# First stage of a fused attention and expert layer on one core: three rounded products in place of plain fp32, value rows spread over the chunks, statistics and norms reordered

## The reference

```
xn = (x - mean) / sqrt(var + 1e-5)
q, k, v = xn @ Wq.T, xn @ Wk.T, xn @ Wv.T          # 16 heads of 16 columns
attn = softmax(q k^T / 16) v                       # all 4096 x 4096 pairs of each head
scores = softmax(xn @ gate_w.T); idx = top2(scores + gate_b)
y = sum over the 2 experts of scores[idx] * expert_idx(xn);  z = shared expert(xn)
expert(x) = silu((x @ w1 + b1) * (x @ w3 + b3)) @ w2 + b2      # 352 hidden columns
out = x + attn + y + z
```

## Time and profile before

| what | value |
|---|---|
| median of 3 runs | 2173.07 us |
| profiled execution, its own time | 2174.21 us |
| its span | 2172.3 us |
| granted TensorE clock, mean | 0.996 of full |
| TensorE (PE) busy | 2152.4 us, 99% |
| ScalarE (ACT) busy | 2009.4 us, 93% |
| VectorE (DVE) busy | 800.5 us, 37% |
| GpSimd (POOL) busy | 246.0 us, 11% |

### The profile page before, as it was taken

The page is one execution under the profiler, slowest core; times in us unless marked ns, Lnnn a source line. Parts: engine busy times, 40 slices in busy tenths (PEclk is TensorE's granted clock), DMA queues, the critical chain, the costliest instruction groups (busy, mean ns, idle before and its releaser), DMA issues.

```text
span 2172.3 us, 37982 instructions
## 1 busy us (share of the span) xinstructions
PE 2152.4 (99%) x15638; PEld 965.2 (44%) x15638; DVE 800.5 (37%) x1515; ACT 2009.4 (93%) x2209; POOL 246.0 (11%) x242
## 2 busy tenths in 40 slices
PE   9999999999999999999999999999999999999998
PEld 4632344444444444444444444444444444444322
DVE  6321143344344334334334434334334334544200
ACT  4599999999999999999999999999999999999998
POOL 0100465610000000000000000000000002223200
PEclk9999999999999999999999999999999999999999
DMA  7671334332222222213132222213213222332120
GB/s 254 206 280 33 91 121 130 100 90 66 63 78 63 76 57 79 78 54 85 48 77 70 77 64 69 78 50 83 75 50 90 63 69 75 105 97 66 57 78 3
DMA packets 223595, 187.24 MB, mean 86 GB/s; under 512 B 112039, under 2 KB 194558, under 8 KB 223166
## 3 DMA queue, kind: packets, MB, share of 16 engines
q1 hardware_dynamic: 211598, 149.41, 24.3%
q0 software_dynamic: 11824, 35.40, 5.0%
HBM read 130.21 MB, written 54.53 MB: 85 GB/s over the span
## 4 chain that ended last, share of the span: by engine, by line
PE 92%; ACT 7%; DVE 1%; DMA 0%; issue 0%; DVEq 0%
PE PS L672 41%; PE PS L659 29%; PE PS L684 12%; ACT probs L866 6%; PE PS L695 6%; PE PS L565 2%; PE PS L602 1%; PE PS L575 0%; DVE stats L972 0%; PE PS L554 0%; DMA resid<-in_x 0%; DVE probs L996 0%; ACT probs L818 0%; DVE o_t L1169 0%; DVE mv L975 0%
## 5 line engine op out<-in xcount | busy, mean ns | idle before, releaser
L866 ACT ACTIVATE probs<-PS 128x1024 f32<-128x1024 f32 x2048 | 1920.0, 1080 | 96.0 <-PE PS L659 81.8
L672 PE MATMUL PS<-probs,v_head 128*32 128x512 f32 x8192 | 1002.8, 601 | 1.1 <-ACT probs L866 0.8
L659 PE MATMUL PS<-q_ring,k_stack 50*128 50x512 f32 x4096 | 741.3, 446 | 7.0 <-ACT probs L866 6.2
L659 PEld LDWEIGHTS PS<-q_ring,k_stack 50*128 50x128 f32 x4096 | 332.6, 185 | 627.2 <-ACT probs L866 569.6
L672 PEld LDWEIGHTS PS<-probs,v_head 128*32 128x32 f32 x8192 | 206.6, 108 | 448.2 <-issue 359.6
L1194 DVE TENSOR_SCALAR gate_in<-PS,bias_sb 128x256 f32<-128x256 f32 x165 | 79.6, 482 | 754.9 <-PE PS L684 739.5
L684 PE MATMUL PS<-x_hi,w_hi 128*128 128x256 f32 (+1 forms) x660 | 201.3, 305 | 0.0
L684 PE MATMUL PS<-x_hi,w_lo 128*128 128x256 f32 (+1 forms) x660 | 186.5, 283 | 0.0
L684 PE MATMUL PS<-x_lo,w_hi 128*128 128x256 f32 (+1 forms) x660 | 185.6, 281 | 0.0
L921 POOL DMA_DIRECT2D slot_y<-y_sb x39 | 27.9, 716 | 1285.1 <-DVE y_sb L1262 1251.6
L684 PEld LDWEIGHTS PS<-x_hi,w_hi 128*128 128x128 f32 (+1 forms) x660 | 118.6, 180 | 60.0 <-issue 60.0
(11 more groups left out here) (137 smaller groups left out, 1098.2 us busy)
## 6 DMA issues: line engine op xcount, KB each, us to landing
w_raw<-in_w SPq DMA_DIRECT2D x110, 352.0 KB
k_stack<-qk_parts SPq DMA_DIRECT2D x120, 128.0 KB
w_raw<-in_w SPq DMA_DIRECT2D x55, 256.0 KB
q_ring<-qk_parts SPq DMA_DIRECT2D x384, 32.0 KB
slot_x<-part_a SPq DMA_DIRECT2D x39, 256.0 KB, 2.3
slot_in<-slot_x SPq DMA_DIRECT2D x156, 64.0 KB, 2.4
slot_y<-y_sb POOLq DMA_DIRECT2D x39, 256.0 KB, 2.5
k_stack<-qk_parts SPq DMA_DIRECT2D x136, 64.0 KB
```

The source lines that it names most:

```text
L659: last = pe.matmul(bank(2 * score_buffer(turn, g) + r), k_stack[rows, kt * P:(kt + 1) * P], q_ring[rows, sweep, i * QC:(i + 1) * QC], star ...
L672: last = pe.matmul(bank(O_BANK)[VW * j:VW * (j + 1), :], v_head[:, kt, :], probs[:, slot, (j % 2) * QC:(j % 2 + 1) * QC], start=(kt == 0), ...
L866: nc.scalar.activation(probs[:, prob_slot(g), :], bank(2 * score_buffer(h, g), 2), ACT.Exp, scale=ENERGY_SCALE).then_inc(s_exp, 1)
```

## The change

**Formats.** Chunk 0 is still projected in fp32 (`first_project`), the keys before chunk 1 is transposed and the queries after it. For chunks 1 to 7, ScalarE writes two copies of each transposed half: rounded (`xh`, a ring of four chunks) and exact (`xfull`, a ring of two); VectorE writes their difference (`xl`, in `tokens_low`). The weights are split once (`wqk_hi`, `wqk_lo`, `wvg_hi`, `wvg_lo`). A projection job is then six fp32r matmuls of 512 columns, the products high times high, high times low, and low times high over two halves of the features, in place of two fp32 matmuls. A pair of value rows is twelve fp32r matmuls of 264 columns in place of four in fp32.

**Order.** Keys come before queries. Chunks 1 to 3 do both; chunks 4 to 7 do keys alone, and their queries come after chunk 7 (`late_queries`). Value pairs 0 to 4 are done in chunks 1 to 3 in banks 0 and 1, which `turn_xn` also uses; pairs 5 to 9 in chunks 4 to 7 in banks 4 and 5; pairs 10 to 15 at the end. Query norms of the two halves of the chunks go to bank 6 and bank 5, and the shift is made and stored by halves. The statistics of group 2 are split in two groups, and statistics and normalisation are put behind the subtractions that other engines wait for.

**Transfers.** Keys and queries are stored separately, 512 KB a part. `xfull` is stored chunk by chunk (eight DMAs of 512 KB) in place of the one of 4 MB. Head 0's queries of the first sweep are loaded after chunk 7; its shift after the queries of chunk 7 are stored and before the flag. ScalarE's copy of pair 12 waits for the stores of the even chunks' queries.

```diff
+FIRST = NCH // 2
+PAIRS = NT // 2
+SIDE_PAIR = 5
+LATE_PAIR = 10
+LN_GROUPS = ((0, 4), (4, 8), (8, 12), (12, 16), (16, 24), (24, NT))
+LN_LOAD = (0, 1, 2, 2, 3, 4)
...
+def pair_bank(n):
+
+    if n < LATE_PAIR:
+        return 0 if n < SIDE_PAIR else 4
+    return 2 * ((n - LATE_PAIR) % 3)
+
+
+def late_bank(m):
+
+    return 2 + m % 3
...
+                sp.wait_ge(s_xt, DT * (c + 1))
+                sp.dma_start(x_rows[:, :, c * QC:(c + 1) * QC], xfull[:, c % 2, :, :]).then_inc(s_xd[c % 2], 16)
+                store_keys(c)
                 if c:
-                    sp.wait_ge(s_store[part_of(c - 1)], stored(c - 1))
+                    sp.wait_ge(s_kst[(c - 1) % 2], stored(c - 1))
                     load_k_chunk(c - 1)
-                if c == QCH:
-                    load_q_rows(0, 0)
-            sp.wait_ge(s_store[part_of(NCH - 1)], stored(NCH - 1))
+                if c < FIRST:
+                    store_queries(c)
+            for half in range(2):
+                sp.wait_ge(s_qst[half], stored(FIRST - 2 + half))
+            load_q_rows(0, 0)
+            store_queries(4)
+            store_queries(5)
+            sp.wait_ge(s_kst[(NCH - 1) % 2], stored(NCH - 1))
             load_k_chunk(NCH - 1)
-            for s in range(NP_):
-                sp.wait_ge(s_s1, s + 1)
-                sp.dma_start(qshift_parts[s].rearrange("h (c t) -> c h t", c=NCH), spart[:, s, :].bitcast(f32)).then_inc(s_sst, 16)
+            store_shift(0)
+            store_queries(6)
+            store_queries(7)
+            sp.wait_ge(s_sst, 16 * NP_)
+            load_q_shift(0, 0, s_q[0])
             sp.wait_ge(s_flag, 1)
             flag = sp.value_load(flag_i[0:1, 0:1], min_val=0, max_val=1)
...
+                    pe.wait_ge(s_xt, dt + 1)
+                    last = pe.matmul(bank(4 - 2 * w + i), wqk[:, w, dt, i * P:(i + 1) * P], cols, start=(dt == 0), stop=(dt == DT - 1))
...
+                hi, lo = xh[c % XRING], xl[c % XRING]
+                for dt in range(DT):
+                    pe.wait_ge(s_xh, DT * c + dt + 1)
+                    pe.matmul(bank(b), wqk_hi[:, w, dt, cols], moving(hi, dt), start=(dt == 0), stop=False)
+                    pe.matmul(bank(b), wqk_lo[:, w, dt, cols], moving(hi, dt), start=False, stop=False)
+                pe.wait_ge(s_xl, c + 1)
+                for dt in range(DT):
+                    last = pe.matmul(bank(b), wqk_hi[:, w, dt, cols], moving(lo, dt), start=False, stop=(dt == DT - 1))
+                last.then_inc(s_qk, 1)
+
+            def keys(c, i):
+
+                if c == 1 and i == 0:
+                    pe.wait_ge(s_wl, 1)
+                pe.wait_ge(s_res, key_job(c - 1) + i + 1)
...
+            def value_rows(n):
+
+                if n == 0:
+                    pe.wait_ge(s_vwl, 1)
+                if n < SIDE_PAIR or n == LATE_PAIR:
+                    pe.wait_ge(s_xt, DT * turned[0])
+                    pe.wait_ge(s_xh, DT * turned[0])
+                if n == SIDE_PAIR:
+                    pe.wait_ge(s_res, query_job(FIRST - 1) + DT)
+                if n == LATE_PAIR + 1:
+                    pe.wait_ge(s_res, NCH * NJ)
+                if n == LATE_PAIR + 2:
+                    pe.wait_ge(s_qn, 2)
+                if 0 < n <= LATE_PAIR:
+                    pe.wait_ge(s_vc, n)
+                if n >= LATE_PAIR + 3:
+                    pe.wait_ge(s_vc, n - 2)
+                for i in range(2):
+                    c, t = (2 * n + i) // TPC, (2 * n + i) % TPC
+                    rows = slice(t * P, (t + 1) * P)
                     for dt in range(DT):
-                        last = pe.matmul(bank(6 + w), hones_b[:, dt, own], sq[:, c % 2, w * DT + dt, :],
-                                         start=(c == 0 and dt == 0), stop=(c == NCH - 1 and dt == DT - 1))
-                last.then_inc(s_nr, 1)
+                        dst = bank(pair_bank(n) + i)[:, 0:VE]
+                        pe.matmul(dst, xh[c % XRING][:, dt, rows], wvg_hi[:, dt, :], start=(dt == 0), stop=False)
+                        pe.matmul(dst, xh[c % XRING][:, dt, rows], wvg_lo[:, dt, :], start=False, stop=False)
+                        last = pe.matmul(dst, xl[c % XRING][:, dt, rows], wvg_hi[:, dt, :], start=False, stop=(dt == DT - 1))
+                last.then_inc(s_v, 1)
...
             turn_first()
+            first_project(1, 0)
+            first_project(1, 1)
+            turn_xn(1)
+            first_project(0, 0)
+            first_project(0, 1)
             pe.wait_ge(s_hb, 2)
-            for c in range(NCH):
-                pe.wait_ge(s_xt, c + 1)
-                project(c, 0)
-                project(c, 1)
+            key_norms(0)
+            for c in range(1, FIRST):
+                keys(c, 0)
+                query_norms(c - 1)
+                keys(c, 1)
+                if c > 1:
+                    value_rows(2 * c - 3)
+                queries(c, 0)
+                turn_xn(c + 1)
+                queries(c, 1)
+                key_norms(c)
+                value_rows(2 * c - 2)
+            for c in range(FIRST, NCH):
+                keys(c, 0)
+                if c == FIRST:
+                    query_norms(FIRST - 1)
                 if c < NCH - 1:
                     turn_xn(c + 1)
-                if c:
-                    norms(c - 1)
-                project(c, 2)
-                project(c, 3)
...
-            value_rows(0)
+                if c == FIRST:
+                    value_rows(5)
+                keys(c, 1)
+                value_rows(c + 2)
+                key_norms(c)
+            late_queries(4, 0)
+            late_queries(4, 1)
             pe.wait_ge(s_mk, 1)
             pe.transpose(bank(7)[0:1, 0:P], kmax[:, 0:1], ident_sb[:, :]).then_inc(s_kt, 1)
-            value_rows(1)
+            late_queries(5, 0)
+            query_norms(4)
+            late_queries(5, 1)
             pe.wait_ge(s_krow, 1)
             pe.matmul(bank(7)[:, P:P + 1], krow[0:1, 0:P], ones_sb[0:1, 0:1], start=True, stop=True).then_inc(s_kb, 1)
-            value_rows(2)
-            value_rows(3)
-            value_rows(4)
+            late_queries(6, 0)
+            query_norms(5)
+            late_queries(6, 1)
+            late_queries(7, 0)
+            query_norms(6)
+            late_queries(7, 1)
+            value_rows(10)
+            query_norms(7)
+            value_rows(11)
             pe.wait_ge(s_gcol, 1)
             pe.transpose(bank(6)[0:1, 0:P], qbound[:, 1:2], ident_sb[:, :]).then_inc(s_grow, 1)
-            for n in range(5, NT // 2):
+            for n in range(12, PAIRS):
                 value_rows(n)
...
+                if n == 12:
+                    act.wait_ge(s_qst[0], stored(6))
...
-            take_xn(0)
+            take_first()
             root(1)
+            act.wait_ge(s_const, 16 * N_CONST)
+            nc.scalar.activation(wqk_hi[:, :, :, :], wqk, ACT.Copy).then_inc(s_wh, 1)
+            split_keys(0, 0)
+            split_keys(0, 1)
+            take_tokens(1)
+            split_queries(0, 0)
+            split_queries(0, 1)
             root(2)
-            for c in range(NCH):
-                split(c, 0)
-                split(c, 1)
-                if c < NCH - 1:
-                    take_xn(c + 1)
-                split(c, 2)
-                split(c, 3)
+            act.wait_ge(s_const2, 16 * N_CONST2)
...
+            for c in range(1, FIRST):
+                split_keys(c, 0)
+                if c == 3:
+                    root(4)
+                split_keys(c, 1)
+                if c > 1:
+                    keep_values(2 * c - 3)
+                split_queries(c, 0)
+                take_tokens(c + 1)
+                split_queries(c, 1)
                 if c == 1:
                     root(3)
-                if c == 3:
-                    root(4)
-            act.wait_ge(s_nr, NCH)
-            nc.scalar.activation(qnorm, bank(6), ACT.Sqrt).then_inc(s_qn, 1)
-            act.wait_ge(s_store[part_of(NCH - 2)], stored(NCH - 2))
-
-            def keep_values(n):
-
-                act.wait_ge(s_v, n + 1)
-                src = bank(2 * (n % 3), 2).rearrange("p (i n) -> p i n", i=2)
-                nc.scalar.activation(v_all[:, 2 * n:2 * n + 2, :], src[:, :, 0:VE], ACT.Copy).then_inc(s_vc, 1)
-
-            keep_values(0)
-            keep_values(1)
+                keep_values(2 * c - 2)
+            for c in range(FIRST, NCH):
+                split_keys(c, 0)
+                if c < NCH - 1:
+                    take_tokens(c + 1)
+                if c == FIRST:
+                    keep_values(5)
+                split_keys(c, 1)
+                if c == FIRST:
+                    root(5)
+                    act.wait_ge(s_nq, FIRST)
+                    nc.scalar.activation(qnorm[0:HALF, :], bank(6)[0:HALF, :], ACT.Sqrt).then_inc(s_qn, 1)
+                keep_values(c + 2)
+            split_queries(4, 0)
+            split_queries(4, 1)
+            split_queries(5, 0)
```

(102 more changed lines are left out.)

243 lines of the change are left out of this document (160 added, 83 removed).

## The result

The changed kernel takes 2178.17 us (median of 20 runs, 2176.13 to 2184.14), the one before 2174.27 (20 runs). The ratio is 1.002, with an interval from 1.0013 to 1.0027: slower by 4 us, where 10.5 us less were forecast. The time lies above the stated range of 2157 to 2170.

A forecast was written before the change was run, and what follows sets the result against it. TensorE was taken to bound the stage before the first exponential. Its work -15.5, start -0.5, stalls +4.0 and handing over +1.5 sum to -10.5: 2163.7 from the profiled 2174.2, put at 2162.6 against the median; range 2157 to 2170.

The forecast's parts named there:

- TensorE's work: Projection stage: a job takes 1.35 us in place of 1.72, a pair 1.46 in place of 1.78; 15.5 us less.
- The rule of the Trainium skill: Weight loads overlap only matmuls of other row groups; by it the stage grows 23 us. Rival of unhidden weights: 2217, chance 0.03.
- The stalls up to 67 us: TensorE's waits in the stage, mainly for normalised rows of chunks 2, 4 and 6; all stalls 8.1 us, 4 us more.
- the layout: The engines' programs laid side by side with unit costs, giving when TensorE reaches each chunk and when SP's queue is free.
- VectorE's unit costs: Stage: 0.69 us per subtraction from PSUM, 1.4 to normalise a chunk, 0.34 per tile of statistics; 4.0 in chunks 4 to 7.
- I take no cost for it; the bound is 5 us: Stage's end: late stores and shift land at 97 to 103 us, TensorE's sum ends at 100.9; no cost counted, at most 5.
- The tail rival: Last stores queue behind head 0's query rows; shift load or pair 12's copy 3 to 5 us late; 2167, chance 0.20.
- The clock: Rival: TensorE's short waits in chunks 1 to 7 lower its clock to 1.2 GHz; 2183 at 40 us, chance 0.07.
- Behind the stage nothing: After the first exponential the programs are the same, so no gain or loss counted; bounds 2 us either way.
- the earlier start: Stage's start: first_project begins after the first half of chunk 0 is copied, not both; 0.5 us less.
- stalls and handing over: TensorE's waits in the stage cost 4 us more, handing over between engines 1.5 more (bounds 0 and 5).

The follow-up runs named there:

- e8: e6 with the first half of the shift stored, and head 0's first-sweep shift loaded, by GpSimd's queue in place of SP's; 2160.46 us, ratio 0.9951.
- e10: e8 with GpSimd's fills back where the change has them, after the key norms of chunk 5; 2168.16 us, ratio 0.9989.
- e1: The changed kernel with GpSimd's fills started after the key norms of chunk 7 in place of chunk 5; 2167.11 us, ratio 0.998.
- e6: e5 with head 0's shift loads issued ahead of the stores of queries 7; 2164.19 us, ratio 0.9975.
- e2: The changed kernel with the wait for the store of queries 6 moved from pair 12's copy to the first exponential; 2176.0 us, ratio 1.0023.
- e5: e1 and e2 together, with head 0's query rows loaded in chunk 5 and the parts of queries 6 in x_full; 2166.58 us, ratio 0.9988.

## Why the prediction was wrong

**TensorE's work: right.** The products of a job in the changed kernel start 0.233 us apart, those of a pair 0.123 (bounds given: 0.213 to 0.236; taken: 0.225 and 0.121):

```profile
21.55 0.40 PE L665 MATMUL PS<-x_parts,wqk_lo 128*128 128x512 f32 x1
21.78 0.39 PE L664 MATMUL PS<-x_parts,wqk_hi 128*128 128x512 f32 x1
22.01 0.39 PE L665 MATMUL PS<-x_parts,wqk_lo 128*128 128x512 f32 x1
```

A job is 1.40 and a pair 1.48, so the saving is 13.8 us, not 15.5. Weights are hidden behind products of all row groups, at 264 and at 512 columns, but for at most 0.02 us a product. The rule of the Trainium skill ("TensorE: Matmul & The Clock Gate", Part 3: Packing small matmuls), named in the prediction, is not borne out here.

**The stalls up to 67 us: right.** TensorE reaches the keys of chunks 1 to 6 at 19.3, 30.6, 41.6, 53.0, 60.4 and 67.4; the layout had 19.5, 30.5, 41.5, 53.1, 60.5 and 67.9. The wait at the transposes of chunk 2 was 1.52 (1.9 forecast), at chunk 4 0.32 (1.3), at chunk 6 0.87 (1.8). With the fills out of the way the layout holds further: in e8 the keys of chunk 7 start at 73.7 and the late queries at 78.3, where it had 73.9 and 78.5.

**VectorE's unit costs: the step that failed.** "1.4 to normalise a chunk" was taken from a stage in which nothing ran beside it. The text said that in chunks 4 to 7 VectorE has 4.0 us of work in 5.5 and counted nothing else. The four instructions took 8.63. GpSimd was left out. Its fills now wait for six chunks' norms in place of seven and start 10 us sooner, while the last normalisation had moved from 62 us to 68. The cost is in e10 against e8: 10.5 us of the start, about 8 of the time. The profile of before showed the fills (8 us on GpSimd from 78 to 86), and that of VectorE's copies and `TENSOR_SCALAR`s only one copy lay beside them, at their end (0.27 us at 86.04). The prediction made nothing of it. Whether the old count of seven would have been enough was not run. In e8 the key norms of chunk 6 end at 74.0 and the last normalisation at 69.1, so the two would not have met there.

**"I take no cost for it; the bound is 5 us": the second failure**, in size. The tail rival named the mechanism (late stores behind query rows, shift load or the copy of pair 12 late) and priced it at 3 to 5; it cost 5.1 on top of the fills, and 7.8 without them. What was too small is the time that SP needs to issue. SP's queue in the changed kernel:

```profile
98.22 0.94 SPq L455 DMA_DIRECT2D qk_parts<-v_all  x2
99.20 2.16 SPq L455 DMA_DIRECT2D qk_parts<-part_q  x2
...
105.08 1.18 SPq L463 DMA_DIRECT2D qshift_parts<-probs  x2
106.30 2.38 SPq L455 DMA_DIRECT2D qk_parts<-probs  x2
108.72 3.16 SPq L455 DMA_DIRECT2D qk_parts<-part_a  x2
111.93 2.88 SPq L432 DMA_DIRECT2D q_ring<-qshift_parts  x4
```

From the first query row (92.70) to the end of the shift load SP needs 22.1 us, and in e1 22.7; the layout had 14.6, from 81.4 to 96.0. The stores of queries 6 and 7 take 5.6 of it (2.0 counted), those of queries 4 and 5 3.1 (2.0), the keys of chunk 7 3.6 (2.6) and the shift load 2.9 (1.2). On top of that comes the landing of the store of queries 6 (6.78), for which the copy of pair 12 waits. The shift's own landing (6.4 in e6) costs SP nothing in the changed kernel, since the stores of queries 6 and 7 take longer to issue. The rows of before held hints: 3.02 us for two stores, and a shift store issued at 95.96 that let the load go at 101.49.

**The clock: right as a mechanism, wrong in its place.** No short wait of 0.3 to 1.5 us lowered it. The one long idle stretch, from 69 to 76.5, did, and TensorE then ran at 1.2 GHz for about 5 us.

**Behind the stage nothing: right.** For the changed kernel the span differs from before by the start of the first exponential, within 0.2 us.

With both faults mended, the ratio is 0.9951, or 10.6 us of 2171; the forecast was 10.5. The saving forecast was there; the fills (8 to 10 us) and the queue (5 to 8) took it, and 4 us more. That the agreement is so close is partly luck. In e8 pair 15 is copied 11.1 us sooner than before: products gave 13.8 (15.5 forecast), the earlier start 1.1 (0.5), and the rest by subtraction, stalls and handing over, took 3.8 (5.5).

## What to carry to other kernels

When a change moves one engine's work in time, lay out every engine that a moved semaphore releases, the idle ones too: GpSimd's fills were free at 78 us and cost 8 to 10 at 68. Read the counts of the waits too, and not only their names. A wait that the profile names is worth only the distance to the next one that ends; mend it together with that one, as e2 alone gave nothing. A value that makes a round trip through DRAM meets the backlog with its store (6.4 us in e6) before its load can start (issued at 104.14, its scores at 107.52), so issue the store as soon as the value is ready, from a queue whose program has nothing else to do first.

## What was not expected of the hardware

- A `TENSOR_SCALAR` from SBUF to SBUF in fp32 stands until a running fill of GpSimd ends (8.63 us for four, after 1.4), though the fill of `k_stack` touches two partitions; reads from PSUM, 8-column tensor-tensor operations and a `TENSOR_SCALAR` of one column beside it are not held (0.69, 0.17 and, in e1 at 86.74, 0.14).
- The issue of a DMA on SP has no fixed length. A key load takes 0.40 to 1.19 us in the kernel before and up to 1.65 in e6, two stores of 512 KB 0.9 to 4.0 (e5, at 99.16). The long ones stand among other large stores; that the backlog causes them is likely and was not shown by itself.
- What stays open: how much of the tail's backlog is due to the stores of `xfull` that the change brought into the stage. A kernel without them was not tried on the chip, as it leaves rows of `xnT_rows` unwritten that are read later.
